# Wavelet attention and top-k experts on one core: triangular ranks, expert tables in groups of 4, 4 and 8, 16-bit digits, a reordered wavelet synthesis and twelve gathers ahead

## The reference, cut to what matters

```python
# x: (2, 1024, 128) f32; TOK = 2048 tokens, D = 128
x = x + attn(layernorm(x))      # Haar-like wavelet, two levels, linear attention on the low band
x = x + ffn(layernorm(x))

# attn: per-channel 4-tap filters h, g; level 1: 1024 -> 512, level 2: 512 -> 256
l1, h1 = dwconv(x, h)[:, ::2], dwconv(x, g)[:, ::2]
l2, h2 = dwconv(l1, h)[:, ::2], dwconv(l1, g)[:, ::2]
low = linear_attention(l2, 16 heads)
for high in (h2, h1):
    low = dwconv(repeat(low, 2), h_synth) + dwconv(repeat(high, 2), g_synth)
attn = layernorm(x + low) * gamma + beta

# ffn: 16 experts, each takes its 256 best tokens (expert choice)
scores = sigmoid(h @ gate_w.T)                      # 2048 x 16
topk_score, topk_ids = top_k(scores.T, 256)         # per expert
eo = (silu(xin @ gw.T + gb) * (xin @ up_w.T + up_b)) @ down_w.T + down_b   # F = 512
out = zeros.at[topk_ids].add(eo * topk_score) + shared_mlp(h)              # shared: 256 wide
```

## Time and profile before

| | us |
|---|---|
| median of 3 runs | 227.01 |
| lowest, highest | 225.34, 230.01 |
| the profiled execution, its own time | 225.88 |
| its span, from the first to the last instruction | 224.1 |

### The profile page before, as it was taken

How to read it: one execution, slowest core, us unless ns; L and a number is a source line. 1 busy time by engine, 2 the same in 40 slices (tenths; PEclk the granted TensorE clock), 3 DMA queues, 4 the chain that set the end, 5 groups by cost and what they waited for, 6 DMA issues and landing times.

```text
span 224.1 us, 3575 instructions
## 1 busy us (share of the span) xinstructions
PE 187.8 (84%) x1188; PEld 162.5 (72%) x1188; DVE 131.1 (58%) x437; ACT 90.1 (40%) x240; POOL 116.8 (52%) x148
## 2 busy tenths in 40 slices
PE   7587999999988989865989999999998998919600
PEld 7556889999954566724879999999987997818500
DVE  4789887569688888899334444444435554312300
ACT  0778402253477567230023444444434454212400
POOL 7600000444106344850777778787877777773550
PEclk9999699999999999996599999999999999997965
DMA  6599999100030171020132323233333333322121
GB/s 175 208 421 420 416 413 419 78 0 3 0 107 0 58 239 48 0 97 0 40 109 56 39 40 50 39 53 49 37 40 45 42 37 40 37 37 23 12 23 12
DMA packets 11616, 22.18 MB, mean 99 GB/s; under 512 B 1488, under 2 KB 8784, under 8 KB 11472
## 3 DMA queue, kind: packets, MB, share of 16 engines
q1 hardware_dynamic: 5968, 17.52, 20.4%
q0 software_dynamic: 5632, 4.46, 14.1%
HBM read 17.65 MB, written 4.33 MB: 98 GB/s over the span
## 4 chain that ended last, share of the span: by engine, by line
PE 47%; DVE 18%; DMA 13%; issue 8%; POOL 6%; ACT 3%; POOLq 1%; SPq 1%; DVEq 0%
DMA out_dram<-area,rows 10%; PE bank L1308 7%; PE bank L1042 7%; PE bank L1309 7%; PE bank L1292 6%; POOL out_dram L465 6%; DVE junk L848 4%; PE bank L998 3%; PE bank L1203 2%; DMA x_tok<-in_x_dram 2%; PE bank L1065 2%; DVE area L910 2%; PE bank L1153 1%; PE bank L1191 1%; PE bank L1247 1%
## 5 line engine op out<-in xcount | busy, mean ns | idle before, releaser
L465 POOL DMA_INDIRECT out_dram<-area,rows x32 | 50.5, 1578 | 20.2 <-ACT area L483 8.0
L643 ACT ACTIVATE sgate<-bank,consts 128x256 f32<-128x256 f32 x64 | 30.3, 473 | 68.9 <-PE bank L1309 68.8
L983 DVE SCALAR_TENSOR_TENSOR area<-bank,consts,sgate 128x256 f32<-128x256 f32 x64 | 30.9, 483 | 44.1 <-ACT sgate L643 44.1
L1292 PEld LDWEIGHTS bank<-wT,area 128*128 128x128 f32 x256 | 38.9, 193 | 3.7 <-DVE area L983 0.4
L453 POOL DMA_INDIRECT hT<-h_rows,rows x32 | 31.7, 989 | 17.4 <-issue 8.8
L1308 PE MATMUL bank<-area,wT 128*128 128x256 f32 x128 | 39.1, 388 | 1.7 <-DVE area L962 1.0
L1292 PE MATMUL bank<-wT,area 128*128 128x128 f32 x256 | 39.3, 277 | 0.2 <-DVE area L983 0.2
L1309 PE MATMUL bank<-area,wT 128*128 128x256 f32 x128 | 38.5, 383 | 0.0
L1309 PEld LDWEIGHTS bank<-area,wT 128*128 128x128 f32 x128 | 24.6, 192 | 3.5
L1308 PEld LDWEIGHTS bank<-area,wT 128*128 128x128 f32 x128 | 20.0, 196 | 2.4 <-issue 2.3
L439 POOL TENSOR_TENSOR sh_hid<-sh_up,sgate 128x128 f32<-128x128 f32 x24 | 10.4, 462 | 21.4 <-ACT sh_up L604 17.1
(11 more groups left out here) (189 smaller groups left out, 268.7 us busy)
## 6 DMA issues: line engine op xcount, KB each, us to landing
wT<-in_weights_dram SPq DMA_DIRECT2D x16, 768.0 KB, 16.4
h_rows<-hrow SPq DMA_DIRECT2D x2, 576.0 KB, 3.3
x_tok<-in_x_dram SPq DMA_DIRECT2D x4, 256.0 KB, 3.9
x_tok<-in_down_b_dram SPq DMA_DIRECT2D x1, 1024.0 KB, 6.1
out_dram<-x SPq DMA_DIRECT2D x4, 256.0 KB, 2.2
hT<-h_rows,rows POOLq DMA_INDIRECT x32, 2.5
out_dram<-area,rows POOLq DMA_INDIRECT x32, 3.3
sh_wT<-in_shared_dram SPq DMA_DIRECT2D x1, 384.0 KB, 3.1
```

The costliest lines, as they stand in the source:

```text
L465: pool.indirect_dma_start(out=out_rows, in_=eo[:, e % 2, c, :], in_offset=None, out_offset=bass.IndirectOffsetOnAxis(ap=rows[:, g, c, k:k ...
L643: act.activation(sgate_e[:, q % SGB, :], up_bank(q)[:, CAP:2 * CAP], ACT.Silu, bias=biasT[:, 1, j, e:e + 1]).then_inc(s_sil, 1)
L983: dve.scalar_tensor_tensor(hidden[:, e % 2, j, :], up_bank(q)[:, 0:CAP], biasT[:, 0, j, e:e + 1], sgate_e[:, q % SGB, :], ALU.add, ALU.mul ...
L1292: last = pe.matmul(bank[3 + e % 2][:, c * P:(c + 1) * P], hidden[:, e % 2, j, c * P:(c + 1) * P], wT[:, e, 2, j, :], start=(j == 0 and c = ...
```

## The change

- Wavelet: the three even matmuls per sequence go. VectorE makes the high-band part of the even positions (`level1_even`, three instructions over both sequences), and `high1` goes behind the first `finish_even`. The odd part of both sequences runs before the transpositions of the attention. The beta of tiles 8 to 11 goes to GpSimd, features of tiles 4 to 7 from VectorE to ScalarE, and the last group is scaled in two halves.
- Search: LOW is 16, so keys are the upper and lower halves of the scores' own words and need no shift or copy (seven rounds and eight). The next base comes from the candidates, so `raise_thr` goes. The router's own sigmoid for the rows goes behind the first count.
- Ranks: no scans. TensorE transposes the two masks and sums them with triangular matrices in token layout.
- Tables: experts 0-3, 4-7 and 8-15. The digits are uint16. The transposition of the table goes; `spread` reads VectorE's product. The tables of experts 8-15 are made within the expert loop, a quarter at a time in steps 1 to 12, and their matmuls in step 13.
- Shared MLP: the last two groups are added by VectorE, the products on GpSimd are 64 wide instead of 128.
- Experts: 12 gathers ahead, two between scatters for eight experts; a trial gather before the first; the transposition of the last expert behind the down projections of the one before.

```diff
-    AHEAD = 13
-    BETWEEN = (2, 2, 2, 2, 2, 2, 1, 1, 1, 1, 1, 1, 1, 0, 0, 0)
-    LOW = 14
+    AHEAD = 12
+    BETWEEN = (2, 2, 2, 2, 2, 2, 2, 2, 1, 1, 1, 1, 0, 0, 0, 0)
+    LOW = 16
...
+        GROUPS = ((0, 4), (4, 4), (8, 8))
...
             pool.wait_ge(s_hstore, 16 * NB)
+            pool.indirect_dma_start(out=trial[:, :], out_offset=None, in_=h_rows[:, :],
+                                    in_offset=bass.IndirectOffsetOnAxis(ap=first_rows[:, 0:1], axis=0),
+                                    ).then_inc(s_trial, 16)
             for chunk in range(AHEAD):
...
+            def level1_even(k, part):
+                return dve.scalar_tensor_tensor(r1p[:, :, 1:N1 + 1:2], h2p[:, :, k:k + N2], tap_sum(1, k), part,
+                                                ALU.mult, ALU.add)
...
+            finish_even(0)
+            for k in range(3):
+                link(high1(k))
+            high1(3).then_inc(s_h1v, 1)
+            finish_even(1)
...
+            dve.wait_ge(s_xna, NB)
+            add_beta(0)
+            add_beta(1)
...
             for r, bit in enumerate(ROUNDS):
...
-                if owed is not None:
-                    link(raise_thr(owed))
                 if bit:
-                    dve.wait_ge(s_dve, step[0])
-                    link(dve.scalar_tensor_tensor(base, ktab, float(1 << (bit - 2)), thr.to_broadcast([P, 3]), ALU.mult, ALU.add))
+                    link(dve.scalar_tensor_tensor(base, ktab, unit * ((1 << (bit - 2)) - (1 << bit)), cand, ALU.mult, ALU.add))
...
-            dve.tensor_tensor_scan(scan_gt, gt, gt, 0.0, ALU.add, ALU.max)
-            link(dve.tensor_tensor_scan(scan_eq, eq, eq, 0.0, ALU.add, ALU.max))
...
+            dve.wait_ge(s_maskT, 2)
+            dve.tensor_copy(mask_T[:, 1, :], bank[7][:, 0:256]).then_inc(s_eqT, 1)
+            dve.wait_ge(s_rank, 2)
+            dve.wait_ge(s_slota, 1)
+            link(dve.tensor_tensor(by_token(slot_u), by_token(slot_a), ranks[1], ALU.max))
+            link(dve.tensor_scalar(slot_h[:, 1, :], slot_u[:, :], HI - 1, None, ALU.bitwise_and))
...
+            link(hot_lo(0, 0, NT))
+            times_token(0, 0, NT)
+            link(dve.tensor_scalar(slot_h[:, 0, :], slot_u[:, :], 4, None, ALU.logical_shift_right))
+            for half in range(2):
+                hot_hi(0, half * NT // 2, (half + 1) * NT // 2)
+            link(hot_lo(1, 0, NT))
+            lay_table(0)
             slot_rows(0)
+            times_token(1, 0, NT)
+            for half in range(2):
+                hot_hi(1, half * NT // 2, (half + 1) * NT // 2)
...
+            add_shared(LAST - 1, bank[4])
+            lay_table(1)
             slot_rows(1)
+            add_shared(LAST, bank[6])
+            keep_x(0)
+            LATER = [(piece, quarter) for piece in (hot_lo, times_token, hot_hi) for quarter in range(4)]
...
             for q in range(E * FT):
+                if q == FINAL:
+                    add_bias(e - 1)
+                    keep_x(e)
...
-                if j == 1 and e > 0:
+                if q == FT or j == 1 and 1 < e < E - 1:
                     add_bias(e - 1)
+                if 1 <= q < 1 + len(LATER):
+                    piece, quarter = LATER[q - 1]
+                    last = piece(2, quarter * NT // 4, (quarter + 1) * NT // 4)
...
-            WARM_T = (0, 8, 8, 0)
-            WARM_1 = 2
-            WARM_I, WARM_E, WARM_S, WARM_L, WARM_C = 0, 0, 6, 3, 10
+            WARM_T = (0, 0, 7, 0)
+            WARM_1 = 10
+            WARM_I, WARM_E, WARM_S, WARM_L, WARM_C = 5, 3, 6, 3, 4
...
+            for k in range(2):
+                pe.wait_ge((s_gtT, s_eqT)[k], 1)
+                pe.matmul(rank[k], lift[:, :], mask_T[:, k, :], start=False, stop=False, skip_group_check=True)
+                pe.matmul(rank[k][:, 0:P], ahead_of[:, :], mask_T[:, k, P:2 * P], start=False, stop=False,
+                          skip_group_check=True)
+                last = pe.matmul(rank[k][:, P:2 * P], until[:, :], mask_T[:, k, 0:P], start=False, stop=True,
+                                 skip_group_check=True)
+                last.then_inc(s_rank, 1)
...
             for q in range(E * FT):
                 e, j = divmod(q, FT)
+                if q == FINAL:
+                    down(q - LAG)
+                    down(q - 1)
+                    turn_x(E - 1)
...
+                if q == 13:
+                    table(2)
+                if q == 16:
+                    spread(2)
```

More of the change, by code:

```diff
@@ L413, in _ @@
             norm_scale(norm_no("x", 0))
             norm_scale(norm_no("x", 1))
+            pool.iota(first_rows[:, :], pattern=[[0, 1]], base=0, channel_multiplier=1,
+                      allow_small_or_imprecise_dtypes=True)
+            pool.wait_ge(s_pick, len(SIZES))
+            for n in SIZES:
+                pool.memset(part[n][:, :, :], 1.0)
+                for c in range(2):
+                    pool.tensor_copy(seat[n][:, c, :], own[n][:, :])
+            link(pool.memset(ones[:, :], 1.0))
@@ L415, in _ @@
+            link(last)
+            for n in SIZES:
+                last = pool.tensor_tensor(by_x[n][:, :], part[n][:, 0, :], part[n][:, 1, :], ALU.add)
+            last.then_inc(s_masks, 1)
+            pool.wait_ge(s_xna, NB)
+            pool.wait_ge(s_r1v, 1)
+            for i in range(8, 12):
+                last = pool.tensor_tensor(x_tok[:, i, :], x_tok[:, i, :], beta_bc, ALU.add)
+            last.then_inc(s_beta, 1)
             sum_scale(0)
@@ L577, in _ @@
             keep_x1T(1)
+            features(range(4, 8)).then_inc(s_hna, 1)
             keep_x1T(2)
@@ L1101, in _ @@
             pe.wait_ge(s_h1a, 1)
-            synth1_even(0)
-            synth1_odd(0, h2p, 9)
+            for b in range(NB):
+                synth1_odd(b, h2p, 6)
             for b in range(NB):
@@ new lines, in _ @@
+            rank_base(1, 1, earlier)
+            for k in range(2):
+                pe.wait_ge((s_gtT, s_eqT)[k], 1)
[5 more added lines that the diff above has]
+                last.then_inc(s_rank, 1)
@@ L1229, in _ @@
             for t in range(4):
                 shared_down(LAST - 1, t)
[L1231 to L1240 removed]
+            shared_up(LAST, 0, 0)
```

478 lines of the change are left out of this document (262 added, 216 removed).

## The result

The changed kernel takes 206.28 us (median of four runs, 205.80 to 206.38) against 226.18 us for the kernel before (four runs, 225.04 to 230.01): a ratio of 0.913, with a 95% interval of 0.908 to 0.919. Ratios in this document compare means and leave out the executions that were slow, over 1.5% above the fastest of their kernel. The forecast was 209.5 us, so it was right in sign and range, and 3.2 us too high. The profiled execution took 206.38 us with a span of 204.6, so the same 1.78 us lie around the span as before, and the whole gain is in the span: 224.1 - 204.6 = 19.5 us against 17.5 forecast.

What follows compares the result with a forecast made beforehand. TensorE and VectorE bound the kernel up to the token numbers, then GpSimd's queue. Terms 4.1 + 3.0 + 6.6 + 2.1 + 1.7 = 17.5 off 224.1 gave 206.6, 208.4 with the 1.78 around it, plus 1.1: 209.5 us; range 204.5 to 217.

Steps and rivals of the forecast that it cites:

- Scores: Start to scores: TensorE's synthesis shortens and VectorE becomes the bound; 4.1 us earlier, bounds 1.5 to 5.
- what I took back for GpSimd's beta: Wavelet: GpSimd's added beta runs beside VectorE's two-input work, which slows it; 0.4 us deducted from the gain.
- Search: Scores to found threshold: earlier first count, shorter seam, no `raise_thr`; 3.0 us earlier, bounds 1.5 to 4.
- Ranks and first tables: Found threshold to first token numbers: 8.0 us instead of 14.6, so 6.6 less, bounds 4.5 to 7.5.
- rival of slow groups of four: Tables: one-hots with innermost runs of 4 cost 1.3 each, 2.0 to 2.5 us more, 212; chance 0.12.
- Numbers to first scatter: First token numbers to first scatter: 12 gathers ahead instead of 13; 2.1 us less, bounds 0 to 3.
- The trial's step: Before the first gather: the hidden trial gather may save the 0.28 us by which that gather exceeds 0.94.
- just inside: Second scatter: expert 1 is weighed and ready 21.9 us behind the numbers, against 22.3 from GpSimd's queue.
- the fourth rival: Expert loop start: first experts not weighed in time, second scatter 1.3 to 1.7 late, 211; within the forecast's 0.60.
- First to last scatter: Expert loop: eight intervals of 6.42 and seven of 5.38, 89.0 against 90.98; 1.7 us less, bounds 4 to -3.
- the cover: Last expert: TensorE's 3 us stop is hidden, since it needs 8.4 or 9.9 us and the chain leaves 10.8.
- The marks: Signs expected in the profile: scores at about 57 us, seam 0.75, gathers 1.25 apart, scatters 6.4 eight times, then 5.4.

Runs made afterwards that it cites:

- The version with the warm TensorE: Changed kernel with 13 gathers ahead, one between scatters for expert 1, and 22 warm matmuls ahead of the last transposition: 206.09 us; with 16 instead: 206.11 us.
- the two kernels on the clock: Changed kernel without the eight warm matmuls and with the synthesis step moved back: 209.63 us; kernel before with the eight warm matmuls alone: 226.36 us.

## Why the prediction was right, and by how much its steps were off

- **Scores (4.1 forecast with bounds of 1.5 to 5, 6.0 measured).** The mechanism was right: three groups on VectorE without a wait, 3.28 and 3.35 us apart (3.38 forecast), and the last in halves. The term was mis-sized, and its upper bound was too low, in the step "VectorE was free at 40.59 - 2.04 = 38.55; it will be at 39.4": it was free at 38.53. That step starts from the attention of the kernel before, and the attention ran at half clock there: eight matmuls took 2.06 us where they now take 1.13. The forecast names no window of that stretch. Undoing the two edits together, the warm matmuls and the synthesis step moved ahead, which the prediction doesn't price either, costs 1.6 us at the scores; in the kernel before, the clock alone is worth 0.6. Of the 1.9 missed, 0.9 lie in that step, 0.3 in the last group in halves (2.04 us instead of 2.3), 0.4 in what I took back for GpSimd's beta, and the rest in pieces of 0.1 to 0.2. That beta did take 3.15 us instead of 1.69 beside VectorE, but ended at 36.06, nine microseconds before the group that needs it.
- **Search (3.0, measured 3.5).** The seam was 0.74 (0.75 forecast). Rounds last 1.69 and 1.72 us instead of 1.86 and 1.77 (67.10 - 55.25 over seven; 81.62 - 67.84 over eight; 76.83 - 61.96 over eight; 90.85 - 78.43 over seven). The 3.5 are some 0.7 ahead of the first count, 0.9 at the seam, 0.3 at the end and 1.7 within the rounds, where the prediction's terms give 1.1. Putting the instruction back costs 0.9, the size forecast for `raise_thr` (0.3 in three rounds); the narrow products are 0.3 more, which the prediction gave nothing.
- **Ranks and first tables (6.6, measured 6.4).** 8.2 us instead of 8.0. Up to the low digit 3.2 (3.0 forecast), and the first one-hot 0.84 (0.65); TensorE came to the table at 5.9 (5.6). Of this stretch in the kernel before, the prediction says that VectorE works without a pause; there is one of 0.49 us ahead of 95.36. No run takes the new ranks or tables back: this largest term is read from the two profiles alone. The rival of slow groups of four is refuted by the 0.68 us of the second one-hot.
- **Numbers to first scatter (2.1, measured 2.8).** Twelve gathers 1.25 us apart, as forecast, beside 16-bit two-input work. The 0.3 us of slip didn't come. The trial's step had the wrong place: the prediction hoped for the 0.28 by which the first gather exceeds 0.94 and took the 0.9 ahead of it as fixed, but the gather still took 1.14 and the gap fell to 0.28, 0.6 less. Expert 0 was weighed in time. Expert 1 was not: forecast "just inside" at 21.9 us behind the numbers, it was there at 22.6. What failed is "14.5 us behind the first matmul": it was weighed 15.4 behind it (96.66 to 112.03). The condition of the fourth rival, TensorE's start at 8.35, didn't occur (it was 6.7), yet a smaller form of its effect did: the second pair is 0.6 late. The pieces of the later tables stand between VectorE's products there, but no run shows that they are the cause.
- **First to last scatter (1.7, measured 0.9).** Eight intervals take 52.0 us (51.4 forecast) because of that second pair, seven take 38.1 (37.7): 5.44 each against 5.38, since the landings vary between 3.18 and 3.42. The wait for the numbers of expert 8 (0.3) didn't come. The stop of 3 us ahead of expert 15 and the stretch at half clock behind it did, and the cover held: weighed at 195.15, scatter at 195.62. The forecast gave 9.9 of 10.8 us; it was 10.3 of 10.7 (from 184.90), a margin of half a microsecond, so that it held was lucky in part. The version with the warm TensorE shows that the half clock costs nothing at the end.
- **The marks.** "First gather 37 to 39 us behind the scores" was wrong (35.0), and didn't follow from the prediction's own terms, which give 27.1 + 8.0 + 0.9 = 36.0. Scores at 57 were missed by the first term. Of the eight intervals of 6.4 the first was 7.03, and of the seven of 5.4 the first was 5.62. The other marks held.
- **The bounds.** The lower bounds of the terms (1.5, 1.5, 4.5, 0 and -3) add up to 4.5 and not to 7.5; the last one was left out, so all terms at their slow ends would give 3 us more than the prediction counted.
- **The frame.** 1.1 us was added since the median of before lay above its profiled execution. For the kernel after it lies 0.1 below; with the 2.0 of the span that makes the 3.2.

What stays open: why a landing of scatters takes 4.6 to 5.2 us now and then, why expert 1 is weighed 0.9 us later than forecast, and how the gain of ranks, tables and the wavelet's new order divides among their parts, since none of these was taken back by itself.

## What to carry to other kernels

Read the granted clock of every stretch that the change touches, not only of the one in doubt: a half-clock stretch in the kernel before is a possible gain (0.6 us here for the clock alone), and a term that doesn't look at the clock has bounds that are too narrow. When the end is set by a chain of transfers that wait for one another's landing, count the issues and the landings first; engines that finish earlier behind such a chain (the late transposition, the warm TensorE, the trial) gave 0.2 us or less. Numbers tuned to one another (gathers ahead, gathers between, when the tables are made) have to be moved together, as the old numbers showed with 2.5 us lost.

## What was not expected of the hardware

- Late landings. In 4 of the 14 profiled executions (the two kernels on the clock, the one with the search instruction, and the late transposition alone) one or two pairs of scatters landed after 4.6 to 5.2 us instead of 3.2 to 3.4, at different experts (7 and 10, 2 and 9, 9, and 10), with nothing in the kernel that differs there. Three of the four profiles are among the four that were taken on one chip, the fourth among the eight on another; the chip of the other two is not on record, and whether the chip has a part in it is not shown. One such landing is 1.3 to 1.9 us, which is of the size of the scatter between runs of one kernel (206.53 to 209.37 without the trial); that it is its cause is only argued.
- The first indirect transfer costs extra: 0.91 us to its start and 1.22 (before) or 1.46 us (without the trial) in it, against 0.28 and 1.14 once a trial has gone ahead, and 0.95 for the gathers behind. The trial itself took 1.48 us, where GpSimd had nothing else to do.
- Four f32 adds on GpSimd take 1.69 us beside VectorE's counts and 3.15 us beside its two-input f32 work, while most of its gathers take 0.95 to 1.02 us beside two-input 16-bit work. The neighbours differ in type, so no run tells whether it is the transfer or the 16-bit work that makes the second almost free.
